# Cross-attention and mixture of experts on one core: the shared FFN moved out of the tile loop, to the head of the expert list

## What is computed

```python
x = x + xattn(layernorm(x), ctx)           # 16 heads of 32, 64 keys, causal mask
xn = layernorm(x)
logits = xn @ router_w.T                   # 8 experts
scores, top_idx = top_k(logits, 2)
moe = sum over the two experts e of scores * (silu(xn @ wg[e]) * (xn @ wu[e])) @ wd[e]
shared = (silu(xn @ sg_w + sg_b) * (xn @ su_w + su_b)) @ sd_w + sd_b
x = x + moe + shared
```

## Time and profile before

| | |
|---|---|
| median of three runs | 942.33 us |
| profiled execution | 941.48 us |
| its span, first to last instruction | 939.8 us |
| TensorE (PE) busy | 818.6 us, 87% |
| VectorE (DVE) busy | 668.8 us, 71% |
| ScalarE (ACT) busy | 446.3 us, 47% |
| GpSimd (POOL) busy | 431.9 us, 46% |
| mean granted clock of TensorE | 0.946 |
| DMA | 81.09 MB, mean 86 GB/s |

### The profile page before, as it was taken

The page is one execution under the profiler, slowest core; times in us unless marked ns, Lnnn a source line. Parts: engine busy times, 40 slices in busy tenths (PEclk is TensorE's granted clock), DMA queues, the critical chain, the costliest instruction groups (busy, mean ns, idle before and its releaser), DMA issues.

```text
span 939.8 us, 19907 instructions
## 1 busy us (share of the span) xinstructions
PE 818.6 (87%) x6538; PEld 520.9 (55%) x6538; DVE 668.8 (71%) x1206; ACT 446.3 (47%) x817; POOL 431.9 (46%) x509
## 2 busy tenths in 40 slices
PE   5659999998999989999898721499999999999995
PEld 2546766666676766667675311255555555555552
DVE  4889898988989989899897349655445555445552
ACT  3545667676766767676674410132223232223221
POOL 1013454544545445455453434345555555555553
PEclk9789999999999999999999755599999999999998
DMA  8203123141131411412111000246666667666671
GB/s 313 90 12 111 58 55 125 69 121 57 46 131 47 141 56 45 131 45 66 44 55 43 35 23 1 57 87 119 112 106 117 121 108 119 114 115 114 113 116 16
DMA packets 36464, 81.09 MB, mean 86 GB/s; under 512 B 8448, under 2 KB 9472, under 8 KB 35008
## 3 DMA queue, kind: packets, MB, share of 16 engines
q0 software_dynamic: 15904, 35.70, 21.7%
q1 hardware_dynamic: 20512, 44.73, 14.5%
HBM read 46.71 MB, written 35.53 MB: 88 GB/s over the span
## 4 chain that ended last, share of the span: by engine, by line
PE 62%; DVE 16%; issue 8%; POOL 6%; ACT 6%; DMA 1%; ACTq 0%; DVEq 0%; POOLq 0%
PE psum L1098 38%; PE psum L1089 11%; PE psum L1159 7%; DVE hid L912 4%; PE psum L1195 3%; PE psum L1173 2%; ACT kv_store L561 2%; ACT xn1T L561 1%; DVE xn1T L728 1%; POOL xy L466 1%; POOL exp_all L450 1%; DVE stats L799 1%; DVE xy L843 1%; POOL probsT L520 1%; POOL gate_up L470 1%
## 5 line engine op out<-in xcount | busy, mean ns | idle before, releaser
L1074 DVE SCALAR_TENSOR_TENSOR hid<-psum,gate_up,attn 128x256 f32<-128x256 f32 x71 | 34.4, 484 | 158.1 <-ACT attn L686 158.1
L543 POOL DMA_INDIRECT out<-w_q,gate_up x71 | 112.5, 1584 | 43.6 <-issue 17.4
L533 POOL DMA_INDIRECT x_in<-normed_tokens,gate_up x71 | 70.6, 994 | 116.0 <-DVE y_w L1071 112.4
L686 ACT ACTIVATE attn<-psum,gate_up 128x256 f32<-128x256 f32 x71 | 33.7, 474 | 165.1 <-PE psum L1098 165.1
L1159 PE MATMUL psum<-xn1T,w_q 128*128 128x128 f16 x1536 | 93.5, 222 | 12.7 <-DVE xy L843 9.8
L1098 PE MATMUL psum<-exp_all,hidT 128*128 x426 | 103.5, 379 | 1.0 <-DVE hidT L1061 1.0
L1098 PE MATMUL psum<-exp_all,xn2T 128*128 x432 | 101.7, 386 | 2.9 <-DVE xn2T L728 2.9
L1159 PEld LDWEIGHTS psum<-xn1T,w_q 128*128 128x128 f16 x1536 | 90.4, 100 | 15.4 <-issue 15.1
L1098 PE MATMUL psum<-exp_all,attnT 128*128 x420 | 96.4, 379 | 0.0
L1098 PE MATMUL psum<-w_sh,xn2T 128*128 128x512 f16 x384 | 89.5, 383 | 3.4 <-DVE xn2T L728 3.4
L1098 PE MATMUL psum<-w_o,attnT 128*128 128x512 f16 x384 | 88.1, 379 | 1.6 <-DVE attnT L894 1.6
(11 more groups left out here) (191 smaller groups left out, 1763.8 us busy)
## 6 DMA issues: line engine op xcount, KB each, us to landing
exp_all<-experts SPq DMA_DIRECT2D x8, 1536.0 KB, 8.1
normed_tokens<-xn SPq DMA_DIRECT2D x32, 260.0 KB, 2.6
x_in<-x SPq DMA_DIRECT2D x32, 256.0 KB, 2.8
out<-xy SPq DMA_DIRECT2D x32, 256.0 KB, 2.0
exp_all<-shared SPq DMA_DIRECT2D x1, 1536.0 KB, 11.2
mag_rows<-magnitudes SPq DMA_DIRECT2D x8, 192.0 KB, 3.8
x_in<-normed_tokens,gate_up POOLq DMA_INDIRECT x71, 3.4
out<-w_q,gate_up POOLq DMA_INDIRECT x71, 4.8
```

The costliest lines, as they stand in the source:

```text
L533: pool.indirect_dma_start(x_in[:, t % 4, :], None, xn_dram, bass.IndirectOffsetOnAxis(gather_at[:, t:t + 1], 0)).then_inc(gathered[t % 4], 16)
L543: pool.indirect_dma_start(out, bass.IndirectOffsetOnAxis(add_at[:, t:t + 1], 0), y[:, t % Y_RING, :], None, bounds_check=TOKENS - 1, oob_i ...
L686: act.activation(silu_g, psum[:, GU_BANK, 0:I], ACT.Silu, scale=gate_scale_at[:, bass.ds(t - 2, 1)]).then_inc(silu_ready, 1)
L1074: dve.scalar_tensor_tensor(hid[:, :], psum[:, GU_BANK, I:2 * I], up_scale_at[:, bass.ds(t - 2, 1)], silu_g, ALU.mult, ALU.mult).then_inc(e ...
```

## The change

- The shared FFN leaves the dense stage. The dense stage stores the turned normed tokens (both fp16 halves, 256 KB a tile) to a DRAM tensor, and `base` (x1 plus bias) to `out`. The 32 tiles become entries 0 to 31 of one list; the 71 slots are entries 32 to 102. A shared entry loads the turned tokens, makes gate/up and down, adds `base` read back from `out`, and stores it.
- Entries begin in the last dense steps, one or two per step. Routing is cut into pieces, one per entry, from entry 10 to 30, and its one-hot tables are made by 16 small fp16 comparisons per quad on VectorE alone.
- In both kinds of entry gate and up weights are the stationary operand, in blocks of 128 columns, and the turned tokens move: 48 matmuls of 128 columns instead of 12 of 512. hid comes out turned, so its own turn goes. Gate and up have separate double-buffered PSUM banks, down as well.
- silu with bias on ScalarE replaces tanh and the two products for the shared FFN.
- AV is one fp32 matmul per pair of heads instead of three fp16 ones; probsT is copied once as fp32 and has no low half.
- The dense parts work 0 to 6 tiles behind; the projection shares a bank with the turn of attn; x is loaded a second time for the residual; the copies of keys and values move from ScalarE to GpSimd.

The core of the diff:

```diff
+LAG = 6
+ROUTE_AT = 10
+HOT_AT = ROUTE_AT + 7
+ENTRIES = T + SLOTS
...
         def over_tiles(eng, step, entry):
...
-            for j in range(behind):
-                step(B + j // TPB, j % TPB)
+            for tile in range(T, T + LAG):
+                step(tile // TPB, tile % TPB)
+                if tile > T:
+                    entry(2 * (tile - T) - 2)
+            for n in range(2 * LAG - 3, ENTRIES + 2):
+                entry(n)
...
+            def load_shared(n):
+                if n >= 4:
+                    sp.wait_ge(up_mm, n - 3)
+                else:
+                    sp.wait_ge((q_mm, scores_mm, av_mm, av_mm)[n], T)
+                sp.wait_ge(xT_stored, 16 * (n + 1))
+                sp.dma_start(xgT[n % 4].rearrange("p v c q -> p (v c q)"), xT_dram[n * P:(n + 1) * P, :]
+                             ).then_inc(shared_in[n % 4], 16)
...
+            def entry(n):
+                if 0 <= n - 3 < T:
+                    store_shared(n - 3)
+                if n < T:
+                    load_base(n)
+                if n + 3 < T:
+                    load_shared(n + 3)
...
+                if j == 1 and live(t2 + 1):
+                    wait(pool, scores_mm, t2 + 1)
...
+                    batch_keys(b)
...
                 if live(t2):
-                    for n in range(2):
-                        dve.wait_ge(probsT_hi, 2 * t2 + n + 1)
-                        low(probsT[:, 1, 4 * n:4 * n + 4, :].rearrange("p r q -> p (r q)"), bank(n), P_UP,
-                            probsT[:, 0, 4 * n:4 * n + 4, :].rearrange("p r q -> p (r q)"), probsT_ready)
...
                     for r in range(PAIRS):
-                        dst = psum[:, r // 4, (r % 4) * 2 * VW:(r % 4 + 1) * 2 * VW]
-                        for a, z in PASSES:
-                            last = pe.matmul(dst, probsT[:, a, r, :], v_bd[:, z, r, :, :].rearrange("p h w -> p (h w)"),
-                                             start=(a == z == 0), stop=(a == 1))
+                        last = pe.matmul(psum[:, r // 4, (r % 4) * 2 * VW:(r % 4 + 1) * 2 * VW], probsT[:, r, :],
+                                         v_bd[:, r, :, :].rearrange("p h w -> p (h w)"), start=True, stop=True)
...
+            def route_hot(quad):
...
+                wait(dve, hot_used, quad - 1)
+                for k in range(2):
+                    for i in range(4):
+                        tok = 4 * quad + i
+                        dve.tensor_scalar(hot_lo[:, quad % 2, k, i, :], iota_p16, lo[:, k, tok:tok + 1], None, ALU.is_equal
+                                          ).then_inc(hot_ready, 1)
+                        dve.tensor_scalar(hot_hi[quad % 2][:, k, i, :], iota_s16, hi[:, k, tok:tok + 1],
+                                          token_no[:, tok:tok + 1], ALU.is_equal, ALU.mult).then_inc(hot_ready, 1)
...
+            def turned(dst, xT, weights, n, done):
+                for o in range(n):
+                    for c in range(C):
+                        for a, z in PASSES:
+                            last = pe.matmul(dst[:, o * P:(o + 1) * P], weights(a, c, o), xT[:, z, c, :],
+                                             start=(c == 0 and a == z == 0), stop=(c == C - 1 and a == 1))
+                last.then_inc(done, 1)
...
+            def entry(n):
+                m, k = n - 1, n - 2
+                t, tm, tk = ranked(n), ranked(m), ranked(k)
...
+                if t is not None:
+                    pe.wait_ge(gathered[t % 4], 16 * (t // 4 + 1))
+                    wait(pe, xgT_ready, t - 1)
+                    transposes(bank(XG_BANK[t % 2]), x_in[:, t % 4, :], C, xg_mm)
+                if elive(m):
...
+                        pe.wait_ge(xgT_ready, tm + 1)
+                        e = expert_now[tm % 2]
+                        turned(bank(GATE_BANK[m % 2]), xgT[m % 4],
+                               lambda v, c, o: expert_part(e, v, c * 2 * I + o * P, P), CI, gate_mm)
+                        turned(bank(UP_BANK[m % 2]), xgT[m % 4],
+                               lambda v, c, o: expert_part(e, v, c * 2 * I + I + o * P, P), CI, up_mm)
+                if elive(k):
+                    pe.wait_ge(hidT_ready, k + 1)
+                    wait(pe, y_ready, k - 1)
...
+                        product(bank(DOWN_BANK[k % 2]), chunks(hidT[:, k % 2]),
+                                lambda v, c: expert_part(e, v, GU + c * H, H), CI, down_mm)
+                if t is not None:
...
+                    expert_now[t % 2] = expert_at(t)
```

More of the change, by code:

```diff
@@ L284, in plain, with over_tiles @@
             eng.sem_inc(waits_met, 1)
-        def over_tiles(eng, step, behind):
+        def over_tiles(eng, step, entry):
             for b in range(2):
@@ L293, in over_tiles, with entry_amid, elive, ranked @@
                     step(b, j)
-            for j in range(behind):
-                step(B + j // TPB, j % TPB)
[L297 to L309, removed]
+            for tile in range(T, T + LAG):
[4 more added lines that the diff above has]
+                entry(n)
+        def entry_amid(tile, entry):
+            if isinstance(tile, int) and tile > T + 1:
+                entry(2 * (tile - T) - 3)
+        def elive(n):
+            return 0 <= n < ENTRIES
+        def ranked(n):
+            return n - T if T <= n < ENTRIES else None
         def found(e):
@@ L435, in inv_std @@
                 pool.wait_ge(ln_var[which], tile + 1)
+                wait(pool, (xn1_ready, xn2_ready)[which], tile)
                 plain(pool)
@@ L477, in step @@
                     low_piece(e, pieces[1])
-            over_tiles(pool, step, 4)
+            for b in range(2):
+                for j in range(TPB):
+                    step(b, j)
+            with pool.Fori(2, B) as b:
+                for j in range(TPB):
+                    step(b, j)
+            for tile in range(T, T + LAG):
+                step(tile // TPB, tile % TPB)
             pool.wait_ge(av_mm, T)
@@ new lines, in step @@
+                if live(t4):
+                    act.wait_ge(attnT_mm, t4 + 1)
+                    copy(flat(attnT[:, 0, :, :]), bank(4), 1.0, attnT_hi)
+                if live(t3):
+                    for n in range(2):
+                        act.wait_ge(probsT_mm, 2 * t3 + n + 1)
+                        copy(probsT_flat[:, 4 * P * n:4 * P * n + 4 * P], bank(n), 1.0, probsT_ready)
+                if live(t5):
+                    act.wait_ge(xn2T_mm, t5 + 1)
+                    wait(act, xT_stored, 16 * t5)
+                    copy(flat(xn2T[:, 0, :, :]), bank(6), X_UP, xn2T_hi)
@@ L696, in _ @@
+            over_tiles(act, step, entry)
         @block.vector
@@ L798, in stage_stats @@
             def stage_stats(which, src, tile):
+                wait(dve, ln_rstd[which], tile)
                 dve.bn_stats(stats[:, which, :], src).then_inc(ln_chain[which], 1)
@@ L1003, in _ @@
-            for n in range(2):
-                hot(n, n)
-            with dve.Fori(1, QUADS // 2) as two:
-                for n in range(2):
-                    hot(2 * two + n, n)
-            dve.wait_ge(hot_used, QUADS)
-            halves = [psum[:, 1, 0:SLOTS], psum[:, 2, 0:SLOTS]]
-            fl = [hid[:, n * SLOTS:(n + 1) * SLOTS] for n in range(3)]
-            link(dve.tensor_scalar(fl[0], halves[1], 0.0, TOKENS / 2.0, ALU.is_gt, ALU.mult))
-            link(dve.tensor_tensor(fl[0], fl[0], halves[1], ALU.add))
@@ L1085, in _ @@
+            dve.wait_ge(const_ready, 2)
+            over_tiles(dve, step, entry)
         @block.tensor
@@ L1217, in step @@
-                if live(t3):
-                    pe.wait_ge(hid_ready, t3 + 1)
-                    wait(pe, attnT_ready, t2 + 1 if live(t2) else T)
-                    product(psum[:, 4, I:I + E], chunks(xn2T), columns(w_r, E), C)
-                    transposes(psum[:, 4, :], hid, CI, hidT_mm)
+                if live(t4):
+                    pe.wait_ge(attnT_ready, t4 + 1)
+                    if isinstance(t4, int) and t4 == 0:
+                        pe.wait_ge(wo_split, 1)
+                    product(bank(4), chunks(attnT), columns(w_o, H), C, proj_mm)
```

875 lines of the change are left out of this document (456 added, 419 removed).

## The result

The changed kernel takes **1024.1 us** (median of 4 runs, 1020.4 to 1024.9) against 941.9 of the kernel before (4 runs, 939.0 to 943.4): ratio 1.087, 95% interval 1.083 to 1.091. The forecast was 1050 us. The profiled execution has a span of 1021.7 us.

A forecast was written before the change was run, and what follows sets the result against it. TensorE's sequencer was to bound expert slots, a ScalarE and GpSimd chain most dense tiles. First x1 76, dense 397, shared entries and routing 128, experts 440, tail 9: span 1050, forecast 1050 us; own range 985 to 1095, 8 in 10 980 to 1100.

The forecast's parts named there:

- Expert slot: Expert stage: 36 address steps at 0.13 us on TensorE's sequencer make a slot 6.2 us; 71 slots take 440 us.
- the load of the expert number: Expert stage, TensorE's sequencer: loading the expert number was taken at its median, 0.83 us a slot.
- Rival (a): Expert stage: the sequencer does not bind, slots take 4.4 us, total 924 us, faster than before; chance 0.11.
- Rival (b): Expert stage: the array, waiting a third of each slot, falls to 1.2 GHz; 8.6 us a slot, about 1220; chance 0.06.
- Rival (c): Shared entries stall on SP's queue, 6 us each instead of 4, total 1110; chance 0.05, including the 81 ns rule.
- Dense stage: Dense tiles: 12.8 us each, bounds 11.3 and 13.7; 31 tile steps take 397 us.
- the chain: Dense stage: exponential, expert piece, low piece, 1/std, xn2, turned halves, scores in series; 12.5 us in three tiles of four.
- Keys on GpSimd: Dense stage: four key copies on GpSimd in one tile of four, 0.6 us each, 2.4 us.
- fp32 AV: Dense stage, TensorE: AV as fp32 matmuls takes 1.8 us a tile, bounds 0.7 and 1.8.
- Shared entries and routing: Between last x1 and expert products: entries of 4.0 us with routing beside them, 128 us, bounds 120 and 145.
- First x1: Start of the kernel: 65.8 plus 14 for the extra lag minus 4, making 76 us.
- Tail: From the last product to the end: 9 us.

The follow-up runs named there:

- e1: Changed kernel with the expert's weights always taken from expert 0 at constant addresses: 927.1 us, ratio 0.986.
- e9: Changed kernel with GpSimd's low half of the second expert piece made in the next tile's step, behind both 1/std: 982.5 us, ratio 1.044.
- e4: Changed kernel with ScalarE's second expert piece in front of the exponential: 1017.8 us, ratio 1.079.
- e6: Changed kernel with wide expert entries, ScalarE's second piece before the exponential, both GpSimd low pieces ahead of keys and base: 947.0 us, ratio 1.007.
- e7: Kernel before with AV in fp32 alone, one pass where there were three: 969.4 us, ratio 1.029.
- e10: Changed kernel with GpSimd's second low piece behind both 1/std of the next tile, and wide expert entries (tokens stationary): 900.0 us, ratio 0.955.
- e12: Kernel before with GpSimd's second low piece behind both 1/std of the next tile: 981.2 us, ratio 1.042.
- e8: Kernel before with the expert's weights at constant addresses of expert 0: 939.7 us, ratio 1.000.

## Why the prediction was right, and where it was not

- **Expert slot** (6.2 forecast, 5.76 measured; 440 and 408 us). The cause is as forecast: constant addresses take it to 4.41, and 36 addresses in the kernel before bring it there too. The number of steps (36) and their distance (0.13 us; median 0.124) were right, 4.7 us in all. The term that was mis-sized is the load of the expert number: I took 0.83 us, the median before, and it is 0.30. That is 0.53 x 71 = 38 us, of which some 6 came back in the rest of the slot; it is the main error of the forecast. Why the load is shorter stays open. My lower bound, 5.5, used 0.30.
- **Rival (a)**, a sequencer that doesn't bind: fell. But its number, 924, is what e1 gives (927): had the addresses been free, the change would have been 1.4% faster (ratio 0.986).
- **Rival (b)**, the clock: fell. It reads 1.00 in every stretch from 600 to 1000 us. With 4.4 us of work in 5.76 the array never fell to 1.2 GHz.
- **Rival (c)**: fell. Shared entries take 3.97 us, and none waits for its loads. The Trainium skill, "TensorE: Matmul & The Clock Gate", section "Back-to-back issue gap", gives about 81 ns a narrow product. The expert entries seem to agree, 3.95/48 = 82 ns. They don't: from fixed addresses, in the shared entries and in e1, the same products go at 56 ns, and the 82 are two address steps for three products (32 x 0.124 = 3.97).
- **Dense stage** (12.8 a tile forecast, 12.92 measured; 397 and 400 us). By tile I had 12.5, 12.5, 11.3 and 12.5 + 1.2 + 2.4 = 16.1, measured are 12.4, 12.4, 10.6 and 16.4. In the first two the chain was right as a chain, as e9 shows: one link of 1.2 us less plus its wait of 0.6, and of 12.4 us 10.6 are left. The tile with keys came out near its number by luck: its chain runs through TensorE's turns and scores, which my sum had not, at a clock that I had not lowered, and the copies cost 3.4 us instead of 2.4. Luck too is that the 0.3 us that I took off the mean of 13.1, for copies overlapping waits, is not seen; the tile without a piece, 0.7 shorter than forecast, stands in for it. What I had not seen is the second path, 0.61 us behind, through GpSimd's own queue: base addition, low piece, 1/std. The forecast's sum does not suffer from it; the expectations of e4 and e6 did.
- **Keys on GpSimd**: 0.6 us each was right (0.60 to 0.61), 0.85 from start to start.
- **fp32 AV**: 1.8 forecast, 1.74 measured; it lay hidden behind the chain in three tiles of four, and e7 shows its cost uncovered. In the tile without a piece TensorE has no idle time (325.45 to 340.72 us), and in e9 and e10 three tiles of four are like that; whether the three fp16 passes would be faster there was not tried.
- **Shared entries and routing** (128 forecast, 132.9 measured): entries as forecast; the eight with one-hot matmuls take 576.57 - 533.50 = 43.1 us from down product to down product, 11 more than eight at 3.97, where I had 6. Most run over by 5.21 - 3.97 = 1.24 us, the first by 4.3.
- **First x1**: 76 forecast, 69.9. The extra lag did not cost the whole tile step of 14 us that I had put in; no run here takes the start apart, and the other versions of the changed kernel have it at 68.9 to 73.1.
- **Tail** 10.6 for 9.

In sum -6 + 3 + 5 - 32 + 2 = -28 of the 1050, and 1021.7 is what the span is. The errors of dense, routing and tail were small and of the other sign.

## What to carry to other kernels

Count the address computations of an instruction sequencer as you count products: an operand whose address depends on a register costs TensorE's queue 0.12 us each time it changes, and an array product of 0.056 us cannot pay that. Making the many-times-addressed operand the moving, wide one keeps such steps few. And before a link of a chain is shortened, look how far behind the next path into the same instruction is; here it was 0.6 us, and the gain was 0.7 us in two tiles of four and no more. In a ring of engines with single buffers, the best place for a step in one queue depends on where its partner stands in the other.

## What the runs showed of the hardware, unexpected

- TensorE's loads of the expert number have a median of 0.83 us in the kernel before, 0.86 in e7 and 0.85 in e12, and 0.30 in the changed kernel and all ten other versions, e10 with the same 4.54 us slot included. e8 has the slot of 4.54 us too, on a TensorE that is busy throughout, and 0.30. It is thus not the slot's length alone; no run here tells what it is.
- The address steps come 124 ns apart in either form and whether the array has work queued or waits for them.
- After 2.17 us of idling at 535 us one group of 48 products took 4.47 us in place of 2.84, and the granted clock from 537 to 542 us reads 0.66. In the dense stage the mean of 0.96 comes from such falls in the tile with keys, behind 3 us of idling. But idling is not all of it: e1 has the same dense stage and TensorE busy 173.7 of the 200 us from 100 to 300, less than the changed kernel's 177.7, and its clock reads 1.00 there. Its pace is (467.5 - 70.8)/31 = 12.80 us a tile for 12.92, so the falls cost some 0.1 us a tile.
